# Graph layer and routed feed-forward on one core: gathered rows kept as two float32r parts, segment products in float32r, a ring of four units

## The reference

```python
def _L0_gnn_ref(x, W1, b1, W2, b2, edge_index):
    dst = edge_index[0]
    nbr = edge_index[1]
    n = x.shape[0]
    agg = jax.ops.segment_sum(x[nbr], dst, num_segments=n)
    cnt = jax.ops.segment_sum(jnp.ones((nbr.shape[0],), x.dtype), dst, num_segments=n)
    mean = agg / jnp.maximum(cnt, 1.0)[:, None]
    return x @ W1.T + b1 + mean @ W2.T + b2
...
edge_index = jnp.stack([src, dst])
x = x + _L0_gnn_ref(_layernorm(x, axis=-1), ...)
x = x + _L0_ffn_ref(_layernorm(x, axis=-1)[None], ...)[0]
```

## Time and profile before

| | us |
|---|---|
| Median of three executions | 2130.99 |
| Profiled execution, its span from first to last instruction | 2132.4 |
| First stage, until the first gather starts | 109.0 |
| Gathers, first start to last end | 109.0 to 1305.6 |
| Last addition of a segment ends | 1334.5 |
| Experts, until the end | 797.9 |

### The profile page before, as it was taken

One profiled execution on the slowest core, in us unless ns is written; L12 is line 12 of the kernel. 1 busy time (PEld: TensorE's weight loads), 2 busy tenths in 40 slices (PEclk: granted clock), 3 DMA queues, 4 the chain that ended last, 5 costly groups with the idle time before them and its releaser, 6 DMA issues.

```text
span 2132.4 us, 39885 instructions
## 1 busy us (share of the span) xinstructions
PE 1813.6 (85%) x10626; PEld 1524.9 (72%) x10626; DVE 1008.5 (47%) x2242; ACT 870.2 (41%) x2525; POOL 1226.8 (58%) x1144
## 2 busy tenths in 40 slices
PE   6867987789767698766677687999999999999997
PEld 4735764577535476555566476899999999999997
DVE  6849866888546686553344347631111111111111
ACT  5802751167311265421111157654444444444443
POOL 1166666677766677766666653344454544544543
PEclk9979998999878898898888777999999999999999
DMA  9223232322323223334444365772444242442421
GB/s 307 85 84 89 76 86 85 92 83 83 91 87 90 86 84 88 88 87 119 116 119 124 91 190 186 245 221 46 109 119 119 35 119 37 117 119 37 117 38 16
DMA packets 113325, 224.32 MB, mean 105 GB/s; under 512 B 27478, under 2 KB 76796, under 8 KB 107318
## 3 DMA queue, kind: packets, MB, share of 16 engines
q0 software_dynamic: 61376, 129.59, 24.3%
q1 hardware_dynamic: 31568, 74.06, 10.1%
q10 hardware_dynamic: 20262, 19.24, 2.9%
HBM read 374.14 MB, written 35.04 MB: 192 GB/s over the span
## 4 chain that ended last, share of the span: by engine, by line
PE 70%; issue 10%; DVE 8%; another core or an unknown queue 4%; ACT 2%; DMA 2%; POOL 2%; DVEq 1%; SPq 0%; POOLq 0%; ACTq 0%
PE bank L1205 21%; PE bank L1240 18%; PE bank L1256 17%; PE bank L997 6%; DVE agg L1856 2%; POOL arena L617 2%; PE bank L1081 2%; PE bank L1043 1%; PE bank L1228 1%; ACT arena L756 1%; DVE arena L1566 1%; DVE arena L1362 1%; PE bank L1115 1%; DVE arena L1331 1%
## 5 line engine op out<-in xcount | busy, mean ns | idle before, releaser
L617 POOL DMA_INDIRECT arena<-ytab,arena x784 | 831.0, 1060 | 367.2 <-issue 216.4
L1205 PE MATMUL bank<-arena 128*128 x2356 | 675.6, 427 | 132.1 <-ACT arena L756 50.9
L1205 PEld LDWEIGHTS bank<-arena 128*128 128x128 f32 x2356 | 470.3, 212 | 244.2 <-issue 180.1
L890 ACT ACTIVATE arena<-bank,agg 128x128 f32<-128x128 f32 x848 | 311.2, 368 | 410.9 <-PE bank L1240 341.5
L756 ACT ACTIVATE arena<-arena 128x1024 f32<-128x1024 f16 x148 | 156.4, 1057 | 704.2 <-DVE arena L1566 494.5
L1856 DVE TENSOR_TENSOR agg<-agg,bank 128x257 f32 x589 | 247.0, 419 | 385.1 <-PE bank L1205 182.1
L1240 PEld LDWEIGHTS bank<-arena,agg 128*128 128x128 f32 x3392 | 396.1, 192 | 5.4 <-ACT arena L890 0.2
L1240 PE MATMUL bank<-arena,agg 128*128 128x128 f32 x3392 | 398.0, 276 | 0.0
L1256 PE MATMUL bank<-agg,arena 128*128 128x256 f32 x1696 | 383.8, 379 | 0.6 <-DMA agg<-in_b 0.6
L650 POOL DMA_INDIRECT out<-arena x106 | 172.4, 1627 | 329.0 <-issue 249.7
L1256 PEld LDWEIGHTS bank<-agg,arena 128*128 128x128 f32 x1696 | 314.0, 190 | 39.4 <-DMA agg<-in_b 1.1
(11 more groups left out here) (265 smaller groups left out, 1508.2 us busy)
## 6 DMA issues: line engine op xcount, KB each, us to landing
agg<-in_w SPq DMA_DIRECT2D x212, 1024.0 KB
agg<-in_b SPq DMA_DIRECT2D x106, 128.0 KB
arena<-ytab,arena POOLq DMA_INDIRECT x784
ytab<-arena SPq DMA_DIRECT2D x12, 512.0 KB, 3.3
arena<-in_xt ACTq DMA_DIRECT2D x24, 256.0 KB
node<-in_x SPq DMA_DIRECT2D x6, 896.0 KB, 12.3
agg<-in_xt SPq DMA_DIRECT2D x6, 896.0 KB, 12.9
out<-node ACTq DMA_DIRECT2D x6, 896.0 KB
```

The source lines that it names most:

```text
L617: pool.indirect_dma_start(out=rows[:, v % RU, h, 0:D], out_offset=None, in_=ytab[:, :], in_offset=bass.IndirectOffsetOnAxis(ap=rowidx[g % ...
L890: act.activation(hT[:, m, :], hidden_bank(j, m)[:, 0:T], ACT.Relu, bias=b1b[:, b, m:m + 1]).then_inc(s_fr, 1)
L1205: mm = pe.matmul(bank[bank_of(n)][:, 0:W], onehot[n // QUAD % 2][:, n % QUAD, h, :], pair[:, h * W:(h + 1) * W], start=(h == 0), stop=(h = ...
```

## The change

Each value of y is now kept as two float32r numbers. ScalarE writes the high part (the product rounded to float32r) as before, and VectorE writes the low part: the same product again less the high part (`keep_y_low`, one instruction per tile of y, with one operand in PSUM). A row of `ytab` is then 2 KB, the low part first, and so is a gathered row; the ring's row has 514 columns, the last two of them ones. The segment product is made in float32r: for each half one product with the high part and the two ones (258 columns), and one with the low part (256 columns), all four accumulating into the first 258 columns of the bank. To make room, the ring has four units (`RU = 4`, `BACK = 2`), `ybuf` shares the memory of the ring and of `onehot`, and the buffers of the last stage lie elsewhere. TensorE's `y_part` waits for the low part of the tile four before (`s_ylow`) where it waited for ScalarE's copy.

```diff
-RU = 8
-BACK = 4
+RU = 4
+BACK = 2
...
-    ytab = nc.dram_tensor("ytab", [NP, D], F32, kind="Internal").ap()
+    ytab = nc.dram_tensor("ytab", [NP, 2 * D], F32, kind="Internal").ap()
...
+        rows_flat = sb("rows", [P, RU * HALVES * WP], F32R)
+        onehot_flat = sb("onehot", [P, 2 * QUAD * HALVES * P], F32R)
...
-                sp.wait_ge(s_y, 4 * j + n)
+                sp.wait_ge(s_ylow, 4 * j + n)
...
-                        pool.indirect_dma_start(out=rows[:, v % RU, h, 0:D], out_offset=None, in_=ytab[:, :],
+                        pool.indirect_dma_start(out=rows[:, v % RU, h, 0:2 * D].bitcast(F32), out_offset=None, in_=ytab[:, :],
...
-                act.activation(ybuf[:, t % YB, :], bank[t % 4][:, 0:D], ACT.Copy, scale=rstd[:, t:t + 1]).then_inc(s_y, 1)
+                act.activation(ybuf[t // 4 % 3][:, t % 4, 1], bank[t % 4][:, 0:D], ACT.Copy, scale=rstd[:, t:t + 1]).then_inc(s_y, 1)
...
+            act.wait_ge(s_yst[2], 16 * 4)
             lanes_widened(0)
...
                 if t >= 4:
-                    pe.wait_ge(s_y, t - 3)
+                    pe.wait_ge(s_ylow, t - 3)
...
                     for h in range(HALVES):
-                        mm = pe.matmul(bank[bank_of(n)][:, 0:W], onehot[n // QUAD % 2][:, n % QUAD, h, :], pair[:, h * W:(h + 1) * W],
-                                       start=(h == 0), stop=(h == HALVES - 1))
+                        lanes, a = onehot[:, n // QUAD % 2, n % QUAD, h, :], h * WP
+                        pe.matmul(bank[bank_of(n)][:, 0:WP - D], lanes, pair[:, a + D:a + WP], start=(h == 0), stop=False)
+                        mm = pe.matmul(bank[bank_of(n)][:, 0:D], lanes, pair[:, a:a + D], start=False, stop=(h == HALVES - 1))
...
+            def keep_y_low(t):
+
+                v.wait_ge(s_y, t + 1)
+                v.scalar_tensor_tensor(out=ybuf[t // 4 % 3][:, t % 4, 0], in0=bank[t % 4][:, 0:D], scalar=rstd[:, t:t + 1],
+                                       in1=ybuf[t // 4 % 3][:, t % 4, 1].bitcast(F32), op0=ALU.mult, op1=ALU.subtract).then_inc(s_ylow, 1)
+
+            def keep_y_low_to(t):
+
+                while low_kept.value() < min(t, NT):
+                    keep_y_low(low_kept.value())
+                    low_kept.up()
...
             for t in range(RT[0] + 1):
+                keep_y_low_to(5 - (-24 * t // (RT[0] + 1)))
                 rank_slot(0, t)
...
             for i in range(PT[0]):
+                keep_y_low_to(FIRST_PLACED[0] - 3 + i)
                 place_tile(0, i)
...
+            keep_y_low_to(NT)
             rows_listed(0)
```

More of the change, by code:

```diff
@@ L10 @@
 F16 = mybir.dt.float16
+F32R = mybir.dt.float32r
 I32 = mybir.dt.int32
@@ L28 @@
 W = D + 1
+WP = 2 * D + 2
 EPS = 1e-5
@@ L241, in gnn_moe @@
         gate_b = sb("gate_b", [P, E])
-        ROOM = 23100
+        rows_flat = sb("rows", [P, RU * HALVES * WP], F32R)
+        rows = rows_flat[:, :].rearrange("p (r h w) -> p r h w", h=HALVES, w=WP)
+        onehot_flat = sb("onehot", [P, 2 * QUAD * HALVES * P], F32R)
+        onehot = onehot_flat[:, :].rearrange("p (b k h m) -> p b k h m", b=2, h=HALVES, m=P)
+        ybuf = [a[:, 0:4 * 2 * D].rearrange("p (u s d) -> p u s d", s=2, d=D)
+                for a in (rows_flat[:, 0:4 * 2 * D], rows_flat[:, 4 * 2 * D:8 * 2 * D], onehot_flat)]
+        ROOM = 16940
         arena = sb("arena", [P, ROOM])
@@ L255, in take16 @@
             return take(-(-n // 2), F16)[:, 0:n]
-        rows_flat = take(RU * HALVES * W)
-        rows = rows_flat.rearrange("p (r h w) -> p r h w", h=HALVES, w=W)
         free_from = room[0]
@@ L285, in gnn_moe @@
         onehot16 = [take16(QUAD * HALVES * P).rearrange("p (k m) -> p k m", m=P) for _ in range(2)]
-        onehot = [take(QUAD * HALVES * P).rearrange("p (k h m) -> p k h m", h=HALVES, m=P) for _ in range(2)]
-        junk = [onehot[k // 8][:, k % 8 // 2, k % 2].bitcast(F16) for k in range(2 * U)]
         rowidx = [take(CHMAX, I32) for _ in range(2)]
         lane2 = [take16(SMAX * HALVES * 2).rearrange("p (k h r) -> p k h r", h=HALVES, r=2) for _ in range(2)]
+        used_to = room[0]
         offs, slot = ([take(SMAX, I32) for _ in range(2)] for _ in range(2))
@@ L303, in gnn_moe @@
         edge_b = take(2)
-        room[0] = 0
-        take(4 * D)
-        ybuf = take(YB * D).rearrange("p (u d) -> p u d", d=D)
-        room[0] = 0
+        room[0] = free_to
+        junk = [take16(D) for _ in range(2 * U)]
+        assert room[0] <= used_to
+        room[0] = free_to
         hT = take(HB * T).rearrange("p (k n) -> p k n", k=HB)
@@ L312, in gnn_moe @@
         ysb = take(2 * TT * D).rearrange("p (b n d) -> p b n d", b=2, n=TT)
-        assert room[0] <= free_from
+        assert room[0] <= used_to
         room[0] = free_from
@@ L375, in gnn_moe @@
         s_w2s, s_w2c = sem("w2_summed"), sem("w2_centred")
-        s_mm, s_y = (sem(n) for n in ("linear_done", "y_copied"))
+        s_mm, s_y, s_ylow = (sem(n) for n in ("linear_done", "y_high_kept", "y_low_kept"))
         s_xt = [sem(f"xt_in{i}") for i in range(NB)]
@@ L606, in _ @@
                 pool.wait_ge(s_yst[b], 16 * (5 if b == 0 else 4))
-            pool.memset(rows[:, :, :, D:W], 1.0).then_inc(s_ones, 1)
+            pool.memset(rows[:, :, :, 2 * D:WP].bitcast(F32), 1.0).then_inc(s_ones, 1)
             for g in G:
@@ L1067, in _ @@
             pe.wait_ge(s_ones, 1)
-            pe.wait_ge(s_y, NT)
+            pe.wait_ge(s_ylow, NT)
             def self_part(t):
@@ L1194, in _ @@
                         m = min(16, SEGS[g] - k)
-                        at = loaded(ENG.PE, slot[g % 2], k, m, (RU - 1) * HALVES * W)
+                        at = loaded(ENG.PE, slot[g % 2], k, m, (RU - 1) * HALVES * WP)
                         upto = [n_units & COUNTS for n_units in loaded(ENG.PE, need[g % 2], k // 2, m // 2, UNIT0[NG])]
@@ L1493, in sums @@
                 v.tensor_reduce(total[:, at], node[:, at, :], AX.X, ALU.add).then_inc(s_sumx, 1)
+            low_kept = Count()
+            def keep_y_low(t):
[6 more added lines that the diff above has]
+                    low_kept.up()
             def reciprocals(i):
```

9 lines of the change are left out of this document (5 added, 4 removed).

## The result

The changed kernel took 2189.43 us (median of 4 runs, 2187.45 to 2195.59), the kernel before on the same chip 2133.76 us (4 runs). The ratio is 1.0259, 95% interval 1.0238 to 1.028. I had said 2102 us, with a range up to 2185; "slower" had a chance of 0.34.

The account below looks back on a forecast made before the run. GpSimd's own gather time was taken to bound the gather stage: 109.0 + 16 (start) + 1066.2 (gathers) + 100 (waiting) + 14.5 (working off) + 797.9 (experts) = 2103.6 us, less 1.4: 2102 us; range 2035 to 2185.

Parts of the forecast that it names:

- The cover of the ring: Gather stage: four places at 2.5 us a unit leave 3.5 us of stall covered, against 13.3 us with eight.
- the rival: GpSimd's gathers waiting for SyncE: the ring of four decides, slower; 200 us of waiting gives 2202 us; chance 0.25.
- The waiting: GpSimd's waiting in the gather stage falls from 130.4 us to 100 us, today's less a quarter.
- The stalls I listed from the earlier trace: Chain from 131.26 to 1279.86 us: 22 pieces of issue or unknown queue over 3.4 us, 127.1 us in all.
- The first stage: Before the first gather: 49 low parts on VectorE add 16 us, so gathers start at 125 us.
- the upper bound: First stage: at most 25 us added, including TensorE's wait for low parts holding back ranking products.
- Gathers on GpSimd: GpSimd's own time per gather stays at 1.06 us with 2 KB rows; bad end 0.1 us more each.
- The transfer: DMA of 2 KB rows: lands 0.52 us later, 3.73 us after the gather's start; rate does not bound.
- Single products at 0.11 us: TensorE's segment products: float32r single passes of 0.11 us, so a segment costs 0.44 us instead of 0.87.
- the lower clock: TensorE in the gather stage: clock may fall, a segment costing about 0.96 us at 1.2 GHz; counted within the waiting.
- my 253 at a full clock: TensorE's segment products: 589 x 0.43 = 253 us less work; only what GpSimd waits for can come back.
- The end: After the last gather: TensorE works off the ring in 14.5 us instead of 28.9; experts stay 797.9 us.

Follow-up runs that it names:

- y_six_banks: Changed kernel with the products of y over six banks instead of four; 2140.37 us, ratio 1.0631 (quick group).
- back1: Changed kernel with BACK at 1 instead of 2, so three units can be in flight; 2079.02 us, ratio 1.0337 (quick group).
- after_again: The changed kernel, unchanged, run again in a quick group; 2159.92 us, ratio 1.0744.
- back1_six_banks: Changed kernel with BACK at 1 and the products of y over six banks; 2056.6 us, ratio 1.0236 (quick group).
- ring8_1kb_f32r: Changed kernel with ring of eight, BACK 4, 1 KB rows, no low parts, high part read twice; 2112.78 us, ratio 0.9963 (slow group).
- ring4_2kb_no_low: Changed kernel without low parts, high part read twice, 2 KB rows and ring of four kept; 2153.62 and 2149.53 us, ratios 1.0166 and 1.0136 (slow groups).
- before: The kernel before, unchanged, as first profiled in a slow group; 2133.76 us beside the changed kernel.
- before_again: The kernel before, unchanged, run again for its profile in a quick group; 2008.29 us.
- halves_in_float16: Changed kernel with both parts of y in float16, 1 KB rows, ring of eight, BACK 4; 2038.3 us, ratio 1.0127 (quick group).
- one_product_a_half: ring8_1kb_f32r with one segment product a half instead of two; 2001.7 us, ratio 0.9938 (quick group).

## Why the prediction was wrong, step by step

**The cover of the ring: failed, and the direction with it.** I put "3.5 us of stall remain covered", from four places at 2.5 us a unit. That counts the whole ring as usable. But SyncE's program waits for the landing of unit v before it releases unit v - 2 (L504 ahead of L499), so GpSimd may only be one unit ahead of the landing. With the prediction's own numbers: the second gather of unit v starts 6.25 us after the start of unit v - 2 and lands 3.73 us later, at 9.98, and the place is wanted at 10.0. The cover was nothing, not 3.5 us, and with 0.43 us of passing on it is below zero; in the round at 601.88 above it is -0.2 us. I had this mechanism in the rival (two units in flight where four were) and priced it by VectorE's stalls instead of by the loop's own length. One more unit in flight takes the waiting away: 154 us in `y_six_banks` and 52 in `back1` in one group, 150 in `after_again` and 53 in `back1_six_banks` in another; this is shown. The rival had the right place and 200 us of waiting; it was 184. That its size came so close is in part luck: in a slow group the late products alone make the kernel before wait 130 us, and in a quick group, without them, the changed kernel waits 150.

**The waiting, 100 us for 184: two terms in one.** I credited TensorE's faster work with a quarter of today's waiting. `ring8_1kb_f32r` measures that credit with the ring as it was: 130 to 114 us, and 0.37% in time. From there the small ring brings 27 us (141), the rows of 2 KB 31 (172); the last 12, up to the 184 of the changed kernel, lie between two groups and stay open. The 130 us were hardly the time of TensorE's products. In a quick group the same kernel, with the same products, waits 6 us. They go with the late products, which the earlier trace rows showed as VectorE's waits (110.6 us) and which I had treated as one more stall for TensorE to catch up after. The stalls I listed from the earlier trace rows are 21 pieces of issue or of an unknown queue with 121.3 us; the 22nd, 5.78 us, is VectorE's sequencer at L1854. That alone changes little.

**The first stage, +16 for +35.7: the term was in the text, but not in the sum.** "TensorE's new wait for the low part holds back ranking products queued behind it, and VectorE waits for those: that is in the upper bound." The upper bound was 25. The chain after shows the back-and-forth at each slot (start us, us, what):

```profile
50.17 0.48 DVE arena L1339
50.65 0.41 DVE onehot L1509
51.06 0.04 issue
51.10 2.89 PE bank L1050 x8
53.99 0.33 PE bank L979
54.32 0.35 PE bank L983
...
54.72 0.04 issue
54.76 0.58 DVE arena L1370
```

VectorE's low part releases a bank, only then two blocks of y (L1050) run, behind them in TensorE's queue the ranking products (L979, L983), and only then VectorE's next reduction can start. VectorE and TensorE take turns where they used to overlap: TensorE waits for L1509 30.3 us in 11 times, VectorE for L983 17.5. `y_six_banks` starts 16.7 us sooner by breaking the turns (15.0 against `after_again`). At the end the list of rows is ready at 141.6 us, 33.0 later than before, and GpSimd still waits until 144.4 for the last store; `ring4_2kb_no_low`, without low parts, starts at 113.3, so the bigger stores alone cost 4 us. What remains, some 15 us, fits the low parts' own time on VectorE, 21.7 us of which some is hidden; that is what I had as the whole, and no run measures it by itself.

**Gathers on GpSimd, 1.06 us each: right.** 1.042 after. Row size does not reach GpSimd.

**The transfer, landing +0.52 us: too small.** It is +0.83 (1.46 to 2.29 us after the issue). The DMA engines' own time grew by less than I took: the queue holds 39.8% of 16 engines' 2193.7 us, 13,970 engine-us for 8291, and shared out over 784 gathers that is 0.45 us more on each engine, not 0.52. What the rest of the delay is, no run shows. The landing as a whole, 3.73 us from the start, was right: 3.71 us is the median of the 196 gathers of `after_again` for which the trace tells it.

**Single products at 0.11 us: right at a full clock, and of no use.** In the stage TensorE had a granted clock of 0.75. The start of the changed kernel's stage:

```profile
152.85 0.58 PE L1213 MATMUL bank<-rows,onehot 128*128 x1 [9.84 <-SPq L504]
153.23 0.41 PE L1214 MATMUL bank<-rows,onehot 128*128 x1
153.44 0.42 PE L1213 MATMUL bank<-rows,onehot 128*128 x1
153.65 0.42 PE L1214 MATMUL bank<-rows,onehot 128*128 x1
```

From 152 to 155 us the granted clock is 0.50, 1.2 GHz, and the last three starts are 0.21 us apart; in `after_again`, at 606.66, 606.78 and 606.90 us, they are 0.12 apart. I called the lower clock no case of its own. In `ring8_1kb_f32r`, at 0.76 instead of 0.87, TensorE's busy time fell by 143 us, 110 less than my 253 at a full clock. It hardly mattered here, because the saving had nowhere to go.

**The end, 14.5 us: right,** and the runs fit the stated reason: every kernel with a ring of four has 809 to 813 us behind the last gather, and every one with eight 820 to 828.

## What to carry to other kernels

When a ring is made smaller, write down the loop that refills it, in the program order of the queue that releases it, and compare its length with the feeding engine's own pace; places in the ring that the order keeps shut are no cover. Before speeding up an engine, ask what its waits end on: GpSimd waited for TensorE by name, but halving its products gave back 16 of 130 us, and the quick groups showed that the product time was not in it. A wait that a view calls `remote` or `issue` can still be a wait for an engine of the same core: look up which semaphore the program waits for there. A wait that ties a second engine to an old buffer belongs in the sum, priced by what is queued behind it.

## What the runs showed of the hardware that was not expected

- The same program takes 2009 to 2012 us in some groups of runs and 2119 to 2134 in others, at the same gather time (1.06 us each). Chip number 11 is in both, so the record does not tie it to the chip. Nearly all of it lies in the gather stage, 1196.6 us for 1073.0. In the slow groups VectorE and SyncE learn of TensorE's finished segment products late (medians of 3.42 us for 0.57 in `before` and `before_again`). The traces differ there too: those of the slow groups hold 16,151 to 18,666 updates of semaphores, those of the quick ones 29,974 to 30,124, for nearly the same programs; so a wait without a releaser in a slow trace can be one whose update was not recorded. The cause of both is open, and nothing was run that would tell. A change can be 2.6% slower in one kind of group and 7.4% in the other.
- The granted clock was lower where TensorE had less work. Over the gather stage it was 0.87 before and 0.76 in `ring8_1kb_f32r`, where a segment is four single products in place of two fp32 ones. Over the whole span, in quick groups, it was 0.953 in `before_again`, 0.872 in `halves_in_float16` and 0.813 in `one_product_a_half`.
- Twice the bytes in a gather land 0.83 us later, with 0.45 us more of each DMA engine's time per gather and 0.62 of the engines' time in use in the stage instead of 0.34.
